# The seven 128x128 projections of a recurrent mixer as one fp32 product each, where three fp32r products of rounded parts stood

## The chip, the cores and the metric

One core of a Trainium2 chip runs the whole kernel. The metric is device time in microseconds of one execution; before the change the median of three runs is 784.83 us (784.66 to 788.44).

## The reference, cut to what matters

`xn` is the layer norm of an input of 16 sequences x 256 tokens x 128 channels. Two branches read it, and the output is `x + s * silu(cur)`.

```
# branch s, the mixer
xx  = prev_token(xn) - xn
lin = lambda mix, W: (xn + xx * mix) @ W.T          # six of these: r, w, k, v, a, g
r, alpha, g = sigmoid(lin(..)); decay = exp(-softplus(lin(..))); k = tanh(lin(..)); v = lin(..)
state = state * decay + alpha * k * v               # a scan over the tokens
mixed = r * state
s   = (group_norm(mixed) * gn_w + gn_b) * g @ W_out.T + b_out      # the seventh product
# branch cur, four rounds of four experts of width 512
for rnd in range(4):
    cw  = top-2 softmax weights of cur @ Wg[rnd] + bg[rnd]
    cur = cur + sum_e cw[e] * (gelu(cur @ W1[e] + b1[e]) @ W2[e] + b2[e])
```

All of it is fp32. The weights of the seven products are 128x128.

## The kernel before, in words

The 4096 tokens are cut into 8 blocks of 512 (two sequences each), with the channels on the partitions. The experts are run in 128 steps: step s is expert s % 4 of turn s // 4, and a turn is one block in one round. One step is `up` (four hidden tiles) and `down` (their sum into one bank). TensorE's program is one loop over the steps: `up(s + 1)`, `down(s)`, then what else belongs to step s (L1220 to L1236).

Each operand of `up` and `down` is an fp32r tensor, and each fp32 product is made of three fp32r products of 512 columns. For `v` and a weight `w`, `v_hi` is `v` rounded to fp32r and `v_lo = v - v_hi`; `mm_high` (L1079, L1080) multiplies `v_hi` by `w_hi` and by `w_lo`, and `mm_low` (L1083) multiplies `v_lo` by `w_hi`, all three into one PSUM bank. So one `up` is 12 matmuls and one `down` is 12. ScalarE takes each of the four hidden banks with a gelu (L465) and rounds pairs of them (L471), VectorE makes their low parts (L759) and weighs a finished `down` into `tmp` (L773), and GpSimd's queue adds `tmp` to `cur` by a DMA (L415).

The mixers lie between the steps. Mixer m (block m) begins at step 15 + 14 m, and `JOB_AT` gives the step within the mixer at which each of its seven products is made: 0 (w), 1 (a), 2 (k), 3 (v), 5 (r), 6 (g), 12 (the output product, J_S). That makes 8 x 7 = 56 products. For each of the first six, `mixer_input` on VectorE makes `xm` (L836, 128x512) and `parts` makes `part_hi` (L822) and `part_lo` (L824) from it; for the seventh, `mixer_gate` makes `gn` (L892), and `parts` splits that. `project` (L1193 to L1206) is TensorE's side and stands at the end of its step: three matmuls into `p_bank` (`pb`), of which the first waits for `part_ready` and `p_empty`, and the third for `part_ready` again. ScalarE takes `p_bank` (L477, L482) and VectorE takes it for v (L846). The parts have two buffers in turn; the weights' parts `pj_hi`, `pj_lo`, `wo_hi` and `wo_lo` are made once, at steps 13 and 14 (`high_mixw`, `low_mixw`), from copies that were loaded into a part of `xn_t` not yet in use. The SyncE queue therefore holds the copy of block 4 into `xn_t` back until `mixw_low`.

Two other uses of TensorE matter below. The router's logits (L1189) are plain fp32 products already: nine batches of two or four matmuls, each 512 columns against a weight of 32 columns, that go to different 32-partition parts of `r_bank`. And the normalised input is turned by fp32 transposes of 128 columns against the full 128-column identity (L1091, L1102).

Of the kernel before, what the change touches and what calls it, by code (L numbers as in the profile page):

```python
# [5 lines left out]
D = 128  # L6
SEQS, LEN = 16, 256
# [4 lines left out]
NB = TOK // BLK  # L12
# [79 lines left out]
def mixer_gated_experts(nc, x, proj_t, mixes, wout_t, chan_vecs, wg, bg, w1, b1, w2, b2, cw_scratch, out):  # L92
# [7 lines left out]
    with ExitStack() as ctx:  # L100
# [13 lines left out]

        w1_hi, w1_lo = sb("w1_hi", [128, E, F], f32r), sb("w1_lo", [128, E, F], f32r)
        w2_hi, w2_lo = sb("w2_hi", [128, E * FT, D], f32r), sb("w2_lo", [128, E * FT, D], f32r)
        pj_hi, pj_lo = sb("pj_hi", [128, 6, D], f32r), sb("pj_lo", [128, 6, D], f32r)
        wo_hi, wo_lo = sb("wo_hi", [128, D], f32r), sb("wo_lo", [128, D], f32r)
        wg_c = sb("wg_c", [128, R, E])

        wg_p = sb("wg_p", [128, R, RP])
# [26 lines left out]


        NG = 4 * GRP  # L150
        xx, xm = sb("xx", [128, 2, LEN]), sb("xm", [128, 2, LEN])
        part_hi, part_lo = sb("part_hi", [128, 2, 2, LEN], f32r), sb("part_lo", [128, 2, 2, LEN], f32r)
        dec, u, kt, rt, gt, st = (sb(n, [128, 2, LEN]) for n in ("dec", "u", "kt", "rt", "gt", "st"))

        st_blk, cen, sq, mn = dec, kt, u, rt
# [14 lines left out]

        w1_raw = cw_b[:, 1, :].rearrange("p (e f) -> p e f", e=E)
        w2_raw = [(th, xr)[e // 2][:, e % 2, :].rearrange("p (t h) -> p t h", h=D) for e in range(E)]
        proj_raw = xn_t[:, 8:11, 1:LEN + 1]
        wo_raw = xn_t[:, 11, 1:D + 1]

        hb = [bank(f"h_bank{i}") for i in range(FT)]
        yb = [bank(f"y_bank{i}") for i in range(2)]
# [11 lines left out]
        b1_loaded, first_turned, first_high = sem("b1_loaded"), sem("first_turned"), sem("first_high")  # L189
        dve_consts = sem("dve_consts")  # L190
        made, gates_padded, edge_zeroed = sem("made"), sem("gates_padded"), sem("edge_zeroed")
        w1_high, w2_high, mixw_high = sem("w1_high"), sem("w2_high"), sem("mixw_high")
        w1_low, w2_low, mixw_low = sem("w1_low"), sem("w2_low"), sem("mixw_low")
        rstd_ready = sem("rstd_ready")
        xn_first, xn_ready = sem("xn_first"), sem("xn_ready")
        xn_copied = sem("xn_copied")
# [60 lines left out]
        def _(sp):  # L257
# [27 lines left out]
                load_x(c)  # L285
            sp.dma_start(vec[:, :], chan_vecs).then_inc(small_loaded, DMA)
            sp.dma_start(mix[:, :], mixes).then_inc(small_loaded, DMA)
            sp.dma_start(proj_raw, proj_t.rearrange("d (k j) -> d k j", k=3)).then_inc(mixw_loaded, DMA)
            sp.dma_start(wo_raw, wout_t).then_inc(mixw_loaded, DMA)

            def copy_block(b):

                if b < BY_PE:
                    sp.wait_ge(p_empty, b + 1)
                else:
                    sp.wait_ge(cur_placed, b - BY_PE + 1)
                sp.wait_ge(edge_zeroed, 1)
                if b == NB // 2:
                    sp.wait_ge(mixw_low, 2)
                sp.dma_start(xn_t[:, 2 * b:2 * b + 2, 1:LEN + 1],  # L300
                             cur[:, block_of(b)].rearrange("p (b t) -> p b t", b=2)).then_inc(xn_copied, DMA)

# [115 lines left out]
        def _(act):  # L418
# [10 lines left out]
                act.wait_ge(w2_loaded[e], DMA)  # L429
                nc.scalar.activation(w2_hi[:, e * FT:(e + 1) * FT, :], w2_raw[e], ACT.Copy).then_inc(w2_high, 1)  # L430

            def high_mixw():
                act.wait_ge(mixw_loaded, DMA * MIXW)
                nc.scalar.activation(pj_hi[:, :, :].rearrange("p (a k) j -> p a (k j)", a=3), proj_raw,
                                     ACT.Copy).then_inc(mixw_high, 1)
                nc.scalar.activation(wo_hi[:, :], wo_raw, ACT.Copy).then_inc(mixw_high, 1)

            def scale_block(b):

                group = [b in blocks for blocks in NORM_GROUPS].index(True)  # L440
# [78 lines left out]
            for s in range(STEPS):  # L519
                if s == 1:  # L520
                    high_w1(3)
                elif s == 8:
                    router_tanh(1)
                elif s == 13:
                    act.wait_ge(small_loaded, DMA * SMALL)
                    high_mixw()
                elif s == 14:
                    router_tanh(2)
                for m, stage in mixers_at(s):
                    take(m, stage)  # L530
                for b, stage in end_stages_at(s):
                    if stage == "tanh" and b < NB - 2:
                        end_tanh(b)

                def between():
                    if s < E - 1:
                        high_w2(s + 1)
                    for b in at_step(NORM_SCALE, s):
                        scale_block(b)
                    for n in at_step(LOGITS_AT, s - 2):  # L540
                        if n >= 3:
                            router_tanh(n)
                    if (NB - 2, "tanh") in end_stages_at(s):
                        end_tanh(NB - 2)

                def late():
                    if s == 0:
                        router_tanh(0)

                if s + 1 < STEPS:  # L550
                    hidden(s + 1, between, late)
# [13 lines left out]
        def _(dve):  # L565
# [73 lines left out]
            def low_w2(e):  # L639
# [1 line left out]
                dve.wait_ge(w2_high, e + 1)  # L641
                nc.vector.tensor_tensor(w2_lo[:, h, :], w2_raw[e], as_f32(w2_hi[:, h, :]),
                                        ALU.subtract).then_inc(w2_low, 1)

            def low_mixw():
                dve.wait_ge(mixw_high, 2)
                nc.vector.tensor_tensor(pj_lo[:, :, :].rearrange("p (a k) j -> p a (k j)", a=3), proj_raw,
                                        as_f32(pj_hi[:, :, :]).rearrange("p (a k) j -> p a (k j)", a=3),
                                        ALU.subtract).then_inc(mixw_low, 1)
                nc.vector.tensor_tensor(wo_lo[:, :], wo_raw, as_f32(wo_hi[:, :]), ALU.subtract).then_inc(mixw_low, 1)  # L650

            def split_first():

# [160 lines left out]
                dve.wait_ge(half_combined, n + 1)  # L814
                nc.vector.tensor_tensor(last, last, part, ALU.add).then_inc(half_added, 1)

            def parts(m, job, src):

                turn = len(JOBS) * m + job
                if turn >= 2:  # L820
                    dve.wait_ge(p_full, BY_PE + turn - 1)
                nc.vector.tensor_scalar(part_hi[:, turn % 2, :, :], src, 1.0, None, ALU.mult).then_inc(part_ready, 1)  # L822
                dve.wait_ge(part_ready, 2 * turn + 1)
                nc.vector.tensor_tensor(part_lo[:, turn % 2, :, :], src, as_f32(part_hi[:, turn % 2, :, :]),  # L824
                                        ALU.subtract).then_inc(part_ready, 1)

            def mixer_input(m, job):

                xs = xn_t[:, 2 * m:2 * m + 2, :]
                if job == J_W:  # L830
                    dve.wait_ge(xn_copied, DMA * (m + 1))
                    link(nc.vector.tensor_tensor(xx[:, :, :], xs[:, :, 0:LEN], xs[:, :, 1:LEN + 1], ALU.subtract))
                k = KINDS[job]
                if len(JOBS) * m + job > 0:
                    dve.wait_ge(part_ready, 2 * (len(JOBS) * m + job))
                link(nc.vector.scalar_tensor_tensor(out=xm[:, :, :], in0=xx[:, :, :], scalar=mix[:, k:k + 1],  # L836
                                                    in1=xs[:, :, 1:LEN + 1], op0=ALU.mult, op1=ALU.add))
                parts(m, job, xm[:, :, :])

            def mixer_values(m):  # L840

# [47 lines left out]
            def mixer_gate(m):  # L889

                dve.wait_ge(p_empty, p_job(m, J_G) + 1)
                link(nc.vector.scalar_tensor_tensor(out=gn[:, :, :], in0=gt[:, :, :], scalar=1.0, in1=gn[:, :, :],  # L892
                                                    op0=ALU.add, op1=ALU.mult))
                parts(m, J_S, gn[:, :, :])

            def end_scaled(b):

# [61 lines left out]
            for s in range(STEPS):  # L959

                if s == 1:
                    split_cur(1)
                elif s == 2:
                    norm_root(NORM_GROUPS[1])
                elif s == 3:
                    norm_stats(NORM_GROUPS[2][0:2])
                elif s == 6:
                    norm_spread(NORM_GROUPS[2])
                    norm_root(NORM_GROUPS[2])
                elif s == 7:  # L970
                    router_scores(1)
                elif s == 8:
                    router_gates(1)
                elif s == 13:
                    router_scores(2)
                elif s == 14:
                    router_gates(2)
                    low_mixw()
                    nc.vector.tensor_scalar(gnw4[:, :], vec[:, 0:1], 0.25, None, ALU.mult)
                    nc.vector.tensor_scalar(gnb2[:, :], vec[:, 1:2], 0.5, None, ALU.mult).then_inc(dve_consts, 1)  # L980
                    dve.wait_ge(dve_consts, 1)
# [95 lines left out]
        def _(pe):  # L1077
# [115 lines left out]
            def project(m, job):  # L1193

                turn = len(JOBS) * m + job
                if turn == 0:
                    pe.wait_ge(mixw_low, 2)
                if job == J_S:
                    w_hi, w_lo = wo_hi[:, :], wo_lo[:, :]
                else:  # L1200
                    w_hi, w_lo = pj_hi[:, KINDS[job], :], pj_lo[:, KINDS[job], :]
                pe.wait_ge(part_ready, 2 * turn + 1)
                pe.wait_ge(p_empty, p_job(m, job))
                mm_high(pb[:, :], w_hi, w_lo, part_hi[:, turn % 2, :, :])
                pe.wait_ge(part_ready, 2 * turn + 2)
                mm_low(pb[:, :], w_hi, part_lo[:, turn % 2, :, :]).then_inc(p_full, 1)  # L1206

            pe.wait_ge(made, 3)
            for _ in range(WARM_UP):
# [71 lines left out]
```

## Time and profile before

| what | before |
|---|---|
| median of 3 runs | 784.83 us (784.66 to 788.44) |
| profiled execution, first to last instruction (span) | 782.9 us |
| granted TensorE clock, mean of the span | 1.000 |
| PE busy | 777.2 us, 99% |
| DVE busy | 689.3 us, 88% |
| ACT busy | 641.1 us, 82% |
| POOL busy | 115.2 us, 15% |

The profiled execution has no device time of its own in the records; beside its span stand the three times of the runs, whose median is 1.9 us above the span. PE is TensorE's matmul row, PEld its weight loads, DVE is VectorE, ACT ScalarE, POOL GpSimd, SP SyncE. The end of a matmul is modelled, and matmuls overlap: durations of 395 ns stand at starts 230 ns apart. What one costs TensorE is read from the starts. "TensorE clock 1.000" is the upper of its two levels, 2.4 GHz.

### The profile page before, as it was taken

Reading aid. Unit: us, or ns where it says so; the run is one execution under the profiler, and the core shown is the slowest. Engines: PE = TensorE matmul, PEld = TensorE weight load, DVE = VectorE, ACT = ScalarE, POOL = GpSimd, SP = SyncE. Lnnn points to the kernel's source line nnn. Section 1 sums busy time; section 2 is a strip of 40 time slices with the busy share of each in tenths; the row PEclk is TensorE's granted clock in tenths of the full one; section 3 lists DMA queues with packets and bytes.
Section 4 is the critical chain, followed back from the end, with each engine's and each line's share of the span. In section 5 each row is a group of like instructions: output and inputs, shape, how many; then the busy total and the mean of one; then the engine's idle time right before and its main releaser. Section 6 shows DMA issues by size and latency. Waiting matters only on the chain.

```text
span 782.9 us, 9951 instructions
## 1 busy us (share of the span) xinstructions
PE 777.2 (99%) x3392; PEld 619.2 (79%) x3392; DVE 689.3 (88%) x1096; ACT 641.1 (82%) x873; POOL 115.2 (15%) x141
## 2 busy tenths in 40 slices
PE   8999999999999999999999999999999999999998
PEld 6778788887888878888788887888877788888887
DVE  7999987899888889879899788987988989988998
ACT  7989888787888877888788877887877878888886
POOL 0122111111111111111111111111111111111110
PEclk9999999999999999999999999999999999999999
DMA  8467572332642416333154322643227434655453
GB/s 267 139 132 182 128 208 50 95 95 41 148 89 62 107 28 163 92 64 88 33 157 107 81 57 41 149 108 96 41 41 175 108 56 107 134 123 122 70 117 71
DMA packets 77010, 81.62 MB, mean 104 GB/s; under 512 B 48800, under 2 KB 54688, under 8 KB 72992
## 3 DMA queue, kind: packets, MB, share of 16 engines
q0 software_dynamic: 18624, 34.61, 25.8%
q1 hardware_dynamic: 57920, 46.11, 19.5%
q8 instruction: 27, 0.44, 0.2%
q10 hardware_dynamic: 416, 0.26, 0.1%
q14 instruction: 23, 0.19, 0.1%
HBM read 41.91 MB, written 3.93 MB: 59 GB/s over the span
## 4 chain that ended last, share of the span: by engine, by line
PE 95%; ACT 2%; DVE 2%; issue 0%; DMA 0%; DVEq 0%
PE h_bank L1079 15%; PE h_bank L1080 15%; PE h_bank L1083 15%; PE y_bank L1152 15%; PE y_bank L1142 15%; PE y_bank L1140 14%; PE p_bank L1079 2%; PE p_bank L1083 2%; PE p_bank L1080 2%; PE r_bank L1189 1%; ACT g L465 1%; ACT g_hi L471 1%; DVE g_lo L759 0%; DMA cur<-in_x 0%; DVE stats L600 0%
## 5 line engine op out<-in xcount | busy, mean ns | idle before, releaser
L465 ACT ACTIVATE g<-h_bank,b_c 128x512 f32<-128x512 f32 x512 | 329.3, 682 | 77.8 <-PE h_bank L1083 77.0
L759 DVE TENSOR_TENSOR g_lo<-g,g_hi 128x1024 fp32r<-128x1024 f32 x256 | 310.0, 1222 | 72.8 <-ACT g_hi L471 71.2
L471 ACT ACTIVATE g_hi<-g 128x1024 fp32r<-128x1024 f32 x256 | 271.8, 1062 | 8.1
L415 POOL DMA_DIRECT2D cur<-tmp x126 | 110.6, 878 | 642.4 <-DVE tmp L773 544.1
L1079 PE MATMUL h_bank<-cur_hi,w_hi 128*128 128x512 f32 x512 | 202.9, 396 | 0.2 <-ACT cur_hi L513 0.2
L1083 PE MATMUL h_bank<-cur_lo,w_hi 128*128 128x512 f32 x512 | 202.2, 395 | 0.0
L1080 PE MATMUL h_bank<-cur_hi,w_lo 128*128 128x512 f32 x512 | 202.1, 395 | 0.0
L1140 PE MATMUL y_bank<-g_hi,w_hi 128*128 128x512 f32 x504 | 196.2, 393 | 0.0
L1142 PE MATMUL y_bank<-g_hi,w_lo 128*128 128x512 f32 x488 | 193.6, 397 | 0.0
L1152 PE MATMUL y_bank<-g_lo,w_hi 128*128 128x512 f32 x504 | 137.9, 395 | 0.1
L1079 PEld LDWEIGHTS h_bank<-cur_hi,w_hi 128*128 128x128 f32 x512 | 96.2, 188 | 26.6 <-issue 3.8
L1083 PEld LDWEIGHTS h_bank<-cur_lo,w_hi 128*128 128x128 f32 x512 | 96.2, 188 | 23.3 <-DVE cur_lo L663 0.2
L1080 PEld LDWEIGHTS h_bank<-cur_hi,w_lo 128*128 128x128 f32 x512 | 96.3, 188 | 22.6
L1152 PEld LDWEIGHTS y_bank<-g_lo,w_hi 128*128 128x128 f32 x504 | 94.6, 188 | 23.1 <-DVE g_lo L759 0.5
L1140 PEld LDWEIGHTS y_bank<-g_hi,w_hi 128*128 128x128 f32 x504 | 94.7, 188 | 22.4 <-issue 0.8
L1142 PEld LDWEIGHTS y_bank<-g_hi,w_lo 128*128 128x128 f32 x488 | 91.7, 188 | 23.0
L773 DVE SCALAR_TENSOR_TENSOR tmp<-y_bank,b_c,cw_b 128x512 f32<-128x512 f32 x126 | 93.6, 743 | 0.0
L836 DVE SCALAR_TENSOR_TENSOR xm<-xx,mix,xn_t 128x512 f32<-128x512 f32 x48 | 35.7, 744 | 0.3
L824 DVE TENSOR_TENSOR part_lo<-xm,part_hi 128x512 fp32r<-128x512 f32 x48 | 33.2, 692 | 1.7
L708 DVE TENSOR_TENSOR cur_lo<-cur,cur_hi 128x512 fp32r<-128x512 f32 x31 | 21.5, 692 | 1.1
L822 DVE TENSOR_SCALAR part_hi<-xm 128x512 fp32r<-128x512 f32 x48 | 20.8, 434 | 1.6
L1079 PE MATMUL p_bank<-part_hi,pj_hi 128*128 128x512 f32 x48 | 19.3, 401 | 0.0
(153 smaller groups left out, 410.5 us busy)
## 6 DMA issues: line engine op xcount, KB each, us to landing
cur<-tmp POOLq DMA_DIRECT2D x126, 256.0 KB, 3.3
cw_b<-cw_scratch SPq DMA_DIRECT2D x31, 1024.0 KB, 5.2
xn_t<-cur SPq DMA_DIRECT2D x8, 256.0 KB, 3.1
cur<-in_x SPq DMA_DIRECT2D x7, 256.0 KB, 5.0
xr<-in_x SPq DMA_DIRECT2D x28, 64.0 KB, 3.4
out<-o SPq DMA_DIRECT2D x28, 64.0 KB, 2.1
xn_scratch<-o POOLq DMA_DIRECT2D x6, 256.0 KB, 3.0
xr<-xn_scratch SPq DMA_DIRECT2D x24, 64.0 KB, 2.5
```

The source lines that it names most:

```text
L415: pool.dma_start(cur[:, block_of(s // E)], tmp[:, s % SUMS, :], accum_op=ALU.add).then_inc(summed, DMA)
L465: nc.scalar.activation(g[:, gb, ft * BLK:(ft + 1) * BLK], hb[ft][:, :], ACT.Gelu_apprx_tanh, bias=b1_c[:, e * FT + ft:e * FT + ft + 1]).th ...
L471: nc.scalar.activation(g_hi[:, gb, h], g[:, gb, h], ACT.Copy).then_inc(g_hi_done, 1)
L759: nc.vector.tensor_tensor(g_lo[:, gb, h], g[:, gb, h], as_f32(g_hi[:, gb, h]), ALU.subtract).then_inc(g_lo_done, 1)
L773: nc.vector.scalar_tensor_tensor(out=tmp[:, s % SUMS, :], in0=yb[s % 2][:, :], scalar=b2_c[:, e:e + 1], in1=cw_b[:, q, e * BLK:(e + 1) * BLK],
L836: link(nc.vector.scalar_tensor_tensor(out=xm[:, :, :], in0=xx[:, :, :], scalar=mix[:, k:k + 1], in1=xs[:, :, 1:LEN + 1], op0=ALU.mult, op1 ...
L1079: nc.tensor.matmul(out_ap, w_hi, v_hi, start=True, stop=False)
L1080: nc.tensor.matmul(out_ap, w_lo, v_hi, start=False, stop=False)
L1083: return nc.tensor.matmul(out_ap, w_hi, v_lo, start=False, stop=True)
L1140: nc.tensor.matmul(yb[b][:, :], w2_hi[:, e * FT + ft, :], hi, start=(ft == 0), stop=False)
L1142: nc.tensor.matmul(yb[b][:, :], w2_lo[:, e * FT + ft, :], hi, start=False, stop=False)
L1152: last = nc.tensor.matmul(yb[b][:, :], w2_hi[:, e * FT + ft, :], g_lo[:, b, ft * BLK:(ft + 1) * BLK], start=False, stop=(ft == FT - 1))
```

## The change

The mixers' weights and inputs stay fp32, and each of the 56 products becomes one matmul instruction on plain fp32 operands. The rounding and subtracting go, on ScalarE and VectorE, with their buffers and two semaphores. `xm` has two buffers in their place, and `mixer_input` waits, before it writes one, for the product that read it last. The weights are loaded straight to `pj` and `wo`, and the copy of block 4 no longer waits for anything of the weights. The seventh product reads `gn` itself.

```
-        xx, xm = sb("xx", [128, 2, LEN]), sb("xm", [128, 2, LEN])
-        part_hi, part_lo = sb("part_hi", [128, 2, 2, LEN], f32r), sb("part_lo", [128, 2, 2, LEN], f32r)
+        xx, xm = sb("xx", [128, 2, LEN]), sb("xm", [128, 2, 2, LEN])
...
-            sp.dma_start(proj_raw, proj_t.rearrange("d (k j) -> d k j", k=3)).then_inc(mixw_loaded, DMA)
-            sp.dma_start(wo_raw, wout_t).then_inc(mixw_loaded, DMA)
+            sp.dma_start(pj[:, :, :].rearrange("p k j -> p (k j)"), proj_t).then_inc(mixw_loaded, DMA)
+            sp.dma_start(wo[:, :], wout_t).then_inc(mixw_loaded, DMA)
...
-                if b == NB // 2:
-                    sp.wait_ge(mixw_low, 2)
...
-            def high_mixw():
...
-            def low_mixw():
...
-            def parts(m, job, src):
-
-                turn = len(JOBS) * m + job
-                if turn >= 2:
-                    dve.wait_ge(p_full, BY_PE + turn - 1)
-                nc.vector.tensor_scalar(part_hi[:, turn % 2, :, :], src, 1.0, None, ALU.mult).then_inc(part_ready, 1)
-                dve.wait_ge(part_ready, 2 * turn + 1)
-                nc.vector.tensor_tensor(part_lo[:, turn % 2, :, :], src, as_f32(part_hi[:, turn % 2, :, :]),
-                                        ALU.subtract).then_inc(part_ready, 1)
...
-                if len(JOBS) * m + job > 0:
-                    dve.wait_ge(part_ready, 2 * (len(JOBS) * m + job))
-                link(nc.vector.scalar_tensor_tensor(out=xm[:, :, :], in0=xx[:, :, :], scalar=mix[:, k:k + 1],
-                                                    in1=xs[:, :, 1:LEN + 1], op0=ALU.mult, op1=ALU.add))
-                parts(m, job, xm[:, :, :])
+                turn = len(JOBS) * m + job
+                if turn >= 2:
+                    dve.wait_ge(p_full, BY_PE + turn - 1)
+                nc.vector.scalar_tensor_tensor(out=xm[:, turn % 2], in0=xx[:, :, :], scalar=mix[:, k:k + 1],
+                                               in1=xs[:, :, 1:LEN + 1], op0=ALU.mult, op1=ALU.add).then_inc(part_ready, 1)
...
-                parts(m, J_S, gn[:, :, :])
...
-                pe.wait_ge(part_ready, 2 * turn + 1)
-                pe.wait_ge(p_empty, p_job(m, job))
-                mm_high(pb[:, :], w_hi, w_lo, part_hi[:, turn % 2, :, :])
-                pe.wait_ge(part_ready, 2 * turn + 2)
-                mm_low(pb[:, :], w_hi, part_lo[:, turn % 2, :, :]).then_inc(p_full, 1)
+                pe.wait_ge(part_ready, turn + 1)
+                pe.wait_ge(p_empty, p_job(m, job))
+                if job == J_S:
+                    nc.tensor.matmul(pb[:, :], wo[:, :], gn[:, :, :], start=True, stop=True).then_inc(p_full, 1)
+                else:
+                    nc.tensor.matmul(pb[:, :], pj[:, KINDS[job], :], xm[:, turn % 2], start=True, stop=True).then_inc(p_full, 1)
```

TensorE's program around the first product (end of step 15, mixer 0, job w), before and then with the change. `y_bank` is the sum of `down(15)`, `h_bank` the first hidden tile of the next `up`.

```order
403 L1152 MATMUL y_bank<-g_lo,w_hi 128x512 [waits g_lo_done]
404 L1152 MATMUL y_bank<-g_lo,w_hi 128x512
405 L1079 MATMUL p_bank<-part_hi,pj_hi 128x512 [waits p_empty,part_ready,mixw_low]
406 L1080 MATMUL p_bank<-part_hi,pj_lo 128x512
407 L1083 MATMUL p_bank<-part_lo,pj_hi 128x512 [waits part_ready]
408 L1079 MATMUL h_bank<-cur_hi,w_hi 128x512 [waits gelu_done]
```

```order
402 L1120 MATMUL y_bank<-g_lo,w_hi 128x512
403 L1120 MATMUL y_bank<-g_lo,w_hi 128x512 [waits g_lo_done]
404 L1120 MATMUL y_bank<-g_lo,w_hi 128x512
405 L1171 MATMUL p_bank<-xm,pj 128x512 [waits p_empty,part_ready,mixw_loaded]
406 L1047 MATMUL h_bank<-cur_hi,w_hi 128x512 [waits gelu_done]
```

The product keeps its place between `down` and the next `up`; three instructions have become one, and one of their waits is gone. Nothing else in TensorE's program moves.

## Rows read from the trace of the kernel before

**Rows 1.** The page: span, busy time by engine, granted TensorE clock in 40 slices.
```profile
span 782.9 us, 9951 instructions
PE 777.2 (99%) x3392; PEld 619.2 (79%) x3392; DVE 689.3 (88%) x1096; ACT 641.1 (82%) x873; POOL 115.2 (15%) x141
...
PEclk9999999999999999999999999999999999999999
```
**Rows 2.** The waits: engine line, waited for: us in total, times, longest us.
```profile
ACT g L465 <- PE h_bank L1083: 77.0, 106, 2.8
DVE g_lo L759 <- ACT g_hi L471: 71.2, 97, 2.9
...
PEld p_bank L1083 <- DVE part_lo L824: 0.7, 2, 0.4
...
PE y_bank L1102 <- DVE o L940: 0.5, 1, 0.5
```
**Rows 3.** The chain in order of time (start us, us, engine, tile, line), plain steps.
```profile
672.75 0.93 PE y_bank L1152 x4
678.35 0.93 PE y_bank L1152 x4
```
**Rows 4.** The timeline, TensorE, a step with a product: start us, us, engine, operation.
```profile
353.17 0.39 PE L1079 MATMUL h_bank<-cur_hi,w_hi 128*128 128x512 f32 x1
...
358.77 0.39 PE L1079 MATMUL p_bank<-part_hi,pj_hi 128*128 128x512 f32 x1
...
359.23 0.40 PE L1083 MATMUL p_bank<-part_lo,pj_hi 128*128 128x512 f32 x1
359.46 0.39 PE L1079 MATMUL h_bank<-cur_hi,w_hi 128*128 128x512 f32 x1
```
**Rows 5.** The logits' line L1189: durations in ns (min/median/max), first and last start.
```profile
L1189 PE MATMUL r_bank<-cur,wg_p x64: 592/605/617, 16.5 to 600.4; 128*32 128x512 f32 x64
```
**Rows 6.** The timeline around the last batch of logits, TensorE.
```profile
598.88 1.10 PE L1152 MATMUL y_bank<-g_lo,w_hi 128*128 128x512 f32 x4
599.92 1.06 PE L1189 MATMUL r_bank<-cur,wg_p 128*32 128x512 f32 x8
600.91 0.50 PE L1079 MATMUL p_bank<-part_hi,wo_hi 128*128 128x512 f32 x1
601.25 0.40 PE L1080 MATMUL p_bank<-part_hi,wo_lo 128*128 128x512 f32 x1
```
**Rows 7.** The same place, the window cut at 600.2 us, with the weight loads.
```profile
599.92 0.16 PEld L1189 LDWEIGHTS r_bank<-cur,wg_p 128*32 128x32 f32 x8 [0.37 <-issue]
599.92 0.64 PE L1189 MATMUL r_bank<-cur,wg_p 128*32 128x512 f32 x4
```
**Rows 8.** The timeline around four fp32 transposes: matmuls, then weight loads.
```profile
12.97 0.39 PE L1083 MATMUL h_bank<-cur_lo,w_hi 128*128 128x512 f32 x1
13.21 0.60 PE L1091 MATMUL p_bank<-ident,o 128*128 128x128 f32 x4
13.56 0.48 PE L1079 MATMUL h_bank<-cur_hi,w_hi 128*128 128x512 f32 x1
13.88 0.39 PE L1080 MATMUL h_bank<-cur_hi,w_lo 128*128 128x512 f32 x1
...
12.97 0.59 PEld L1091 LDWEIGHTS p_bank<-ident,o 128*128 128x128 f32 x4
```
**Rows 9.** The groups by line and form: xcount, busy us, mean ns.
```profile
L824 DVE TENSOR_TENSOR part_lo<-xm,part_hi 128x512 fp32r<-128x512 f32 x48 | 33.2, 692 | 1.7
...
L822 DVE TENSOR_SCALAR part_hi<-xm 128x512 fp32r<-128x512 f32 x48 | 20.8, 434 | 1.6
```
**Rows 10.** The timeline, ACT, around one product of mixer 5.
```profile
456.66 0.60 ACT L477 ACTIVATE kt<-p_bank 128x512 f32<-128x512 f32 x1 [0.86 <-PE p_bank L1083]
```
**Rows 11.** The timeline, where TensorE waits for a part (mixer 6, job w).
```profile
611.74 0.75 DVE L836 SCALAR_TENSOR_TENSOR xm<-xx,mix,xn_t 128x512 f32<-128x512 f32 x1
...
613.01 0.19 PEld L1079 LDWEIGHTS p_bank<-part_hi,pj_hi 128*128 128x128 f32 x1 [0.42 <-DVE part_hi L822]
```

More of the change, by code:

```diff
@@ L116, in mixer_gated_experts @@
         w2_hi, w2_lo = sb("w2_hi", [128, E * FT, D], f32r), sb("w2_lo", [128, E * FT, D], f32r)
-        pj_hi, pj_lo = sb("pj_hi", [128, 6, D], f32r), sb("pj_lo", [128, 6, D], f32r)
-        wo_hi, wo_lo = sb("wo_hi", [128, D], f32r), sb("wo_lo", [128, D], f32r)
+        pj, wo = sb("pj", [128, 6, D]), sb("wo", [128, D])
         wg_c = sb("wg_c", [128, R, E])
@@ L172, in mixer_gated_experts @@
         w2_raw = [(th, xr)[e // 2][:, e % 2, :].rearrange("p (t h) -> p t h", h=D) for e in range(E)]
-        proj_raw = xn_t[:, 8:11, 1:LEN + 1]
-        wo_raw = xn_t[:, 11, 1:D + 1]
         hb = [bank(f"h_bank{i}") for i in range(FT)]
@@ L191, in mixer_gated_experts @@
         made, gates_padded, edge_zeroed = sem("made"), sem("gates_padded"), sem("edge_zeroed")
-        w1_high, w2_high, mixw_high = sem("w1_high"), sem("w2_high"), sem("mixw_high")
-        w1_low, w2_low, mixw_low = sem("w1_low"), sem("w2_low"), sem("mixw_low")
+        w1_high, w2_high = sem("w1_high"), sem("w2_high")
+        w1_low, w2_low = sem("w1_low"), sem("w2_low")
         rstd_ready = sem("rstd_ready")
@@ L430, in high_w2 @@
                 nc.scalar.activation(w2_hi[:, e * FT:(e + 1) * FT, :], w2_raw[e], ACT.Copy).then_inc(w2_high, 1)
-            def high_mixw():
[L433 to L436, printed above, removed]
             def scale_block(b):
@@ L525, in _ @@
                     act.wait_ge(small_loaded, DMA * SMALL)
-                    high_mixw()
                 elif s == 14:
@@ L643, in low_w2 @@
                                         ALU.subtract).then_inc(w2_low, 1)
-            def low_mixw():
[L646 to L650, printed above, removed]
             def split_first():
@@ L891, in mixer_gate @@
                 dve.wait_ge(p_empty, p_job(m, J_G) + 1)
-                link(nc.vector.scalar_tensor_tensor(out=gn[:, :, :], in0=gt[:, :, :], scalar=1.0, in1=gn[:, :, :],
-                                                    op0=ALU.add, op1=ALU.mult))
-                parts(m, J_S, gn[:, :, :])
+                nc.vector.scalar_tensor_tensor(out=gn[:, :, :], in0=gt[:, :, :], scalar=1.0, in1=gn[:, :, :],
+                                               op0=ALU.add, op1=ALU.mult).then_inc(part_ready, 1)
             def end_scaled(b):
@@ L977, in _ @@
                     router_gates(2)
-                    low_mixw()
                     nc.vector.tensor_scalar(gnw4[:, :], vec[:, 0:1], 0.25, None, ALU.mult)
@@ L1196, in project @@
                 if turn == 0:
-                    pe.wait_ge(mixw_low, 2)
+                    pe.wait_ge(mixw_loaded, DMA * MIXW)
+                pe.wait_ge(part_ready, turn + 1)
+                pe.wait_ge(p_empty, p_job(m, job))
                 if job == J_S:
-                    w_hi, w_lo = wo_hi[:, :], wo_lo[:, :]
+                    nc.tensor.matmul(pb[:, :], wo[:, :], gn[:, :, :], start=True, stop=True).then_inc(p_full, 1)
                 else:
-                    w_hi, w_lo = pj_hi[:, KINDS[job], :], pj_lo[:, KINDS[job], :]
-                pe.wait_ge(part_ready, 2 * turn + 1)
-                pe.wait_ge(p_empty, p_job(m, job))
-                mm_high(pb[:, :], w_hi, w_lo, part_hi[:, turn % 2, :, :])
-                pe.wait_ge(part_ready, 2 * turn + 2)
-                mm_low(pb[:, :], w_hi, part_lo[:, turn % 2, :, :]).then_inc(p_full, 1)
+                    nc.tensor.matmul(pb[:, :], pj[:, KINDS[job], :], xm[:, turn % 2], start=True, stop=True).then_inc(p_full, 1)
             pe.wait_ge(made, 3)
```

## The prediction

> **What bounds the kernel now.** I read the page first, then the waits, the chain, and the timeline at four places. The page [rows 1] has TensorE busy for 777.2 of 782.9 us and its granted clock full in every slice, so it runs at its upper level of 2.4 GHz throughout. Busy time alone proves little, since matmuls overlap in the trace. The waits [rows 2] settle it: the largest wait of ScalarE's gelu is 77.0 us on `up`'s last product, and the largest of VectorE's is 71.2 us on ScalarE, which itself waited for TensorE. TensorE's own waits are the other way round: outside the warm-up at the start the largest is 0.5 us, and its weight loads waited 0.7 us for `part_lo` in the whole run. Everything waits for TensorE, and TensorE for almost nothing.
>
> What it does in that time is regular. A plain step is 5.60 us (672.75 to 678.35, [rows 3]), which is 24 matmuls 0.233 us apart. A step with a product is 6.29 us (353.17 to 359.46, [rows 4]), and the product takes the 0.69 of difference, 358.77 to 359.46: three fp32r matmuls 0.23 us apart, with no gap on either side. So the kernel's time is a sum of TensorE's start-to-start distances. 128 steps at 5.60 are 716.8 us, and 56 products at 0.69 are 38.6 us; the rest of the 782.9 us is nine batches of logits, the start and the end. Whatever lengthens a product lengthens the kernel by 56 times that.
>
> **The change, part by part.**
>
> *The products on TensorE.* 56 x 3 fp32r matmuls go, 56 x 0.69 = 38.6 us. 56 plain fp32 ones of 512 columns against a full 128x128 weight come. The trace has no such product. Its nearest relation is the logits' matmul: plain fp32 and 512 columns too, but against 32 columns of weight. It tells two things. First, one instruction of the program leaves two records: 32 logits matmuls are x64 [rows 5], and a batch of four is x8 [rows 6]. Second, how far apart the two passes start. The last of the eight ends at 599.92 + 1.06 = 600.98 and took 0.59, so it started at 600.39. The last of the first four ends at 599.92 + 0.64 = 600.56 [rows 7] and took 0.617 [rows 5], so it started at 599.94. The distance is 0.45 us, against 0.23 for an fp32r matmul of as many columns: two passes, each at about half the rate. I take 2 x 0.45 = 0.90 us a product, 0.21 more than now, or 56 x 0.21 = **+11.8 us**.
>
> The bounds of a pass: a pass's record is 0.592 long without a load ahead of it [rows 5] and an fp32r matmul's is 0.39 [rows 4], so 0.23 + 0.20 = 0.43 from below; twice the fp32r distance, 0.46, from above. That is 0.86 to 0.92 a product and +9.5 to +12.9 us.
>
> The Trainium skill ("FP8 and Floating Point Precision", section on TensorE precision notes) says that true fp32 takes four passes through the array. The trace shows two records, not four; with four passes at the fp32r distance of 0.23 the sum would be 4 x 0.23 - 0.69 = 0.23 more a product, 12.9 us, which is the upper bound above, so rule and rows speak alike against this change, which leaves three.
>
> *The edges of a product.* Here the shapes part company. Around a batch of logits TensorE loses more than the two passes. The last matmul ahead of it starts at 598.88 + 1.10 - 0.39 = 599.59, so the next was due at 599.82; the logits start at 599.92. After them the first fp32r matmul starts at 600.91 and the second at 601.25, 0.34 later instead of 0.23 [rows 6]: its weight load was not drawn ahead of the running matmul, and 0.11 of it lies open. The loads of the logits were not drawn ahead either: they begin with the matmul, after 0.37 us in which the load row was idle "for nothing" [rows 7]. All in all the batch takes 601.02 - 599.82 = 1.20 us. The fp32 transposes, with a full 128-column weight, lose nothing of this kind [rows 8]: the load starts with the last fp32r matmul at 12.97, the first transpose follows at 13.21, and after four of them the stream is back in step (13.88 - 0.23 = 13.65, so 0.44 us for four). The open edges thus belong either to the 32-column weight or to the fp32 passes. The shape is that of the transposes, so I take none.
>
> The Trainium skill ("TensorEngine Tiling (Array Packing)", section on key properties) states that changing the tiling mode drains the array. By that rule the logits' edges come from their 32-column tiles, and a 128x128 product has none; without it the price would be that of the second rival below.
>
> *VectorE.* For each of 48 products 0.434 + 0.692 us go [rows 9], 54 us in all, and as much each for the 8 output products, 9 us; also one subtraction of the weights. VectorE is ahead of TensorE and only waits longer for ScalarE [rows 2]: nothing. The exception is a place where TensorE waits for a part: at 613.01 its load waited 0.42 us for `part_hi` though `xm` was ready at 611.74 + 0.75 = 612.49 [rows 11]; with the 0.7 us for `part_lo` [rows 2] that is 1.1 us in three waits. A load can be drawn 0.23 us ahead, so about 1.1 - 3 x 0.23 = 0.4 us of it cost time. These go, since `xm` alone is ready earlier: **-0.4 us**, between 0 and -1.1.
>
> *The new wait of VectorE.* It now waits for product n-2 before it writes `xm`, as it did before it wrote `part_hi`. That product ended at least a step, 5.60 us, earlier. The `g_lo` behind it in the queue sees nothing. Nothing.
>
> *ScalarE and SyncE.* Two roundings of weights go. ScalarE takes `p_bank` after 0.86 us of waiting for TensorE [rows 10]; the product ends 0.21 us later, so the wait is 1.07, and the next gelu's bank, which TensorE fills only after the product, moves by as much. Nothing. The copy of block 4 and the gate transfers queued behind it on SP are freed from a wait; none of them is what TensorE waits for. Nothing. If the cover were gone, the 0.6 us of taking `p_bank` would be what came late.
>
> *The sum.* 11.8 - 0.4 = +11.4 us on the profiled span, 794.3 us; on the median of 784.83 (1.9 us above the span, which stays), **796.2 us**. The bounds together are +9.5 - 1.1 = 8.4 to +12.9, or 793.2 to 797.7 us.
>
> **The rivals.**
>
> *The edges come with fp32* (no full-tile rule, as at the logits). Then a product costs 1.20 - 0.02 (the four of a batch start 0.02 apart in all) = 1.18 us, or 0.08 more where the open load ahead of it is of 128 columns (0.11) and not of 32 (0.617 - 0.592 = 0.03): 0.49 to 0.57 more than now, 27 to 32 us, 812 to 816 us. For it: mode and length are those of the logits. Against it: the transposes.
>
> *Only one load lies open.* Each product pays 0.11 us for a load that cannot be drawn ahead on one side: 6.2 us on top, 802.4 us. Nothing shows it but the logits' far edge.
>
> *Full-rate passes, the other side.* Half rate may belong to the 32-column weight, and a full 128x128 fp32 pass may start 0.23 us after another as the fp32r ones do. Then a product is 0.46, which is 0.23 less than now, at each of the 56 places at the end of a step: -12.9 - 0.4, 771.5 us. It decides from 0.345 us a pass (0.69 / 2) downwards. For it: no row shows half rate in an fp32 instruction with a full-width weight. Against it: the transposes, 0.11 us apart for 128 columns [rows 8], are as slow as half rate would make them (0.45 / 4), though their loads could be the cause of that; and the width of a weight gives no reason for the rate of the moving columns.
>
> *Nearly nothing.* Passes of 0.31 to 0.38 us would give a time within 0.5% of now, which is about what a measurement of this kernel can tell from no change. No row has such a distance. That the change does not do what it says is excluded by the program's order: one matmul stands where three stood.
>
> **How the numbers follow.** Forecast 0.74; edges with fp32 0.11; one open load 0.07; full-rate passes 0.05; nearly nothing 0.03. The range takes the forecast's bounds and the open load (0.81 together), with a little for the medians: 792.5 to 803.0 us. Slower by over 0.5% (above 788.8) are the first three, 0.92; within it 0.03; faster (below 780.9) 0.05.
>
> **What would show it.** Right: two records of `p_bank<-xm,pj` for each product, x96 and x16 with the output products, their starts about 0.45 us apart; a step with a product 6.5 us long and a plain one still 5.60; the weight load of the first pass starting with the matmul before it; DVE busy near 625 us and PE still 99%. Wrong: first `up` matmul after a product more than 0.95 us after the product's first record (edges), the second `up` matmul 0.34 after the first (an open load), or passes 0.23 apart (faster). Plain steps of another length would make the whole sum wrong.

## The result, and the profile after

| | before | after |
|---|---|---|
| median of four runs each | 784.79 us (784.66 to 788.44) | 791.87 us (791.85 to 793.41) |
| ratio, 95% interval | | 1.0089 [1.0067, 1.0111] |
| span of the profiled execution | 782.9 us | 790.0 us |

The change costs 7.1 us. Its sign was forecast, its size was not: 11.4 us had been predicted, and 791.87 lies just under the range of 792.5 to 803.0. TensorE's granted clock stayed at its upper level, 0.999 to 1.000 in every run of this document.

The page of the changed kernel, answering to [rows 1]:

```profile
span 790.0 us, 9668 instructions
PE 784.8 (99%) x3336; PEld 610.7 (77%) x3336; DVE 629.2 (80%) x982; ACT 639.9 (81%) x871; POOL 113.4 (14%) x141
...
PEclk9999999999999999999999999999999999999999
```

VectorE lost 60.1 us of work and the kernel is slower. Its waits (engine line, waited for: total us, times, longest) show where the 60 us went, against [rows 2]:

```profile
DVE g_lo L739 <- ACT g_hi L459: 138.8, 139, 3.5
...
ACT g L453 <- PE h_bank L1051: 78.0, 106, 3.0
PEld h_bank L1047 <- issue: 17.3, 61, 0.8
...
PEld h_bank L1048 <- issue: 13.4, 56, 0.2
```

VectorE now waits 138.8 us for ScalarE instead of 71.2. The wait for `part_lo` is gone, and no wait for `xm` has come in its place. New are 56 idle stretches "for nothing" in the row of weight loads ahead of each of the first two matmuls of `up` (the kernel before had 5, 3.8 us in all): a pass of an fp32 product takes 0.43 us, longer than the 0.23 from one load to the next elsewhere, and the load row stands idle meanwhile.

One product, TensorE's timeline (start us, us, engine, operation), answering to [rows 4]:

```profile
366.96 1.09 PE L1120 MATMUL y_bank<-g_lo,w_hi 128*128 128x512 f32 x4
367.89 1.02 PE L1171 MATMUL p_bank<-xm,pj 128*128 128x512 f32 x2
368.35 0.80 PE L1047 MATMUL h_bank<-cur_hi,w_hi 128*128 128x512 f32 x1
368.98 0.39 PE L1048 MATMUL h_bank<-cur_hi,w_lo 128*128 128x512 f32 x1
```

and its loads:

```profile
367.66 0.42 PEld L1171 LDWEIGHTS p_bank<-xm,pj 128*128 128x128 f32 x2
368.32 0.19 PEld L1047 LDWEIGHTS h_bank<-cur_hi,w_hi 128*128 128x128 f32 x1 [0.24 <-issue]
```

The first pass's load begins at 367.66, 0.23 ahead of the product, and the second's at 367.66 + 0.42 - 0.19 = 367.89, ahead of its own pass at 368.32, so no load lies open on the near side. On the far side the row of the first `up` matmul misleads: it is put at 368.35 with 0.80 us, twice its usual length. I read it as queueing behind the second pass: the matmul behind it starts at 368.98, one distance of 0.23 after a start of the first at 368.75, and e2 bears the reading out. So the product took 368.75 - 367.89 = 0.86 us in the stream. In 52 of the 56 products the second pass starts 0.428 to 0.434 us after the first; in the four that follow a batch of logits it is 0.533, the 0.11 of open load that the first fp32r matmul behind the logits pays in the kernel before too [rows 6].

### The profile page after: what moved, and what is told of

It is laid out like the page before. It is cut to its first block, busy times and chain, and to the rows that moved or that the text cites. A ratio compares the mean times of both kernels' runs of the same rounds, so it can differ in the third digit from the quotient of the medians.

```text
span 790.0 us, 9668 instructions
## 1 busy us (share of the span) xinstructions
PE 784.8 (99%) x3336; PEld 610.7 (77%) x3336; DVE 629.2 (80%) x982; ACT 639.9 (81%) x871; POOL 113.4 (14%) x141
## 4 chain that ended last, share of the span: by engine, by line
PE 95%; ACT 2%; DVE 2%; issue 0%; DMA 0%; DVEq 0%
PE h_bank L1047 15%; PE h_bank L1051 14%; PE h_bank L1048 14%; PE y_bank L1120 14%; PE y_bank L1108 14%; PE y_bank L1110 14%; PE p_bank L1171 5%; PE r_bank L1157 1%; PE p_bank L1169 1%; ACT g L453 1%; ACT g_hi L459 1%; DVE g_lo L739 0%; DMA cur<-in_x 0%; DVE stats L587 0%; ACT o L436 0%
## 5 line engine op out<-in xcount | busy, mean ns | idle before, releaser
L739 DVE TENSOR_TENSOR g_lo<-g,g_hi 128x1024 fp32r<-128x1024 f32 x256 | 311.0, 1223 | 141.1 <-ACT g_hi L459 138.8
L1047 PE MATMUL h_bank<-cur_hi,w_hi 128*128 128x512 f32 x512 | 225.1, 440 | 0.2 <-ACT cur_hi L501 0.2
L409 POOL DMA_DIRECT2D cur<-tmp x126 | 108.7, 863 | 651.6 <-DVE tmp L753 499.8
L1171 PE MATMUL p_bank<-xm,pj 128*128 128x512 f32 x96 | 49.3, 595 | 0.0
L1171 PEld LDWEIGHTS p_bank<-xm,pj 128*128 128x128 f32 x96 | 17.9, 189 | 6.5 <-issue 2.5
L686 DVE TENSOR_SCALAR cur_hi<-cur 128x512 fp32r<-128x512 f32 x31 | 13.5, 434 | 0.5
```

What stands on the lines that cost most here:

```text
L409: pool.dma_start(cur[:, block_of(s // E)], tmp[:, s % SUMS, :], accum_op=ALU.add).then_inc(summed, DMA)
L739: nc.vector.tensor_tensor(g_lo[:, gb, h], g[:, gb, h], as_f32(g_hi[:, gb, h]), ALU.subtract).then_inc(g_lo_done, 1)
L1047: nc.tensor.matmul(out_ap, w_hi, v_hi, start=True, stop=False)
L1171: nc.tensor.matmul(pb[:, :], pj[:, KINDS[job], :], xm[:, turn % 2], start=True, stop=True).then_inc(p_full, 1)
```

## The experiments

Each batch ran beside the kernel before, whose median was 784.88 us for e1 to e4, 784.65 for e5 to e11 and 784.75 for e12 to e15.

### e1: VectorE's work put back

```
+                dve.wait_ge(part_ready, turn + 1)
+                link(nc.vector.tensor_scalar(spare_hi[:, :, :], src, 1.0, None, ALU.mult))
+                Own.n += 1
+                nc.vector.tensor_tensor(spare_lo[:, :, :], src, as_f32(spare_hi[:, :, :]), ALU.subtract).then_inc(dve_step, 1)
...
+                spare_parts(turn, xm[:, turn % 2])
...
+                spare_parts(len(JOBS) * m + J_S, gn[:, :, :])
```

> The changed kernel with VectorE's old work put back beside it: it still rounds each product's input and subtracts (128x512, 56 times each) into two spare buffers that nobody reads. TensorE still makes one fp32 product. Theory A (only TensorE's own sum counts; VectorE's relief was worth at most the waits for parts, 0.4 to 0.6 us): 791.9 to 792.5 us, plain steps inside the mixers 5.58 us as in the changed kernel. Rival B (the lighter VectorE is why plain steps inside the mixers fell from 5.60 to 5.58 us and the product's steps cost 0.02 less than two passes): those steps go back to 5.60 and the time rises by 1.5 to 2.5 us, to 793.5 us or more.

Measured: 792.17 us, ratio to before 1.0097 [1.0082, 1.0112], against 1.0089 without that work. VectorE is as full as it was:

```profile
span 790.5 us, 9780 instructions
...
PE 784.7 (99%) x3336; PEld 610.0 (77%) x3336; DVE 688.1 (87%) x1094; ACT 639.7 (81%) x871; POOL 115.3 (15%) x141
```

Theory A held. 59 us of VectorE's work bring 0.3 us here, which these runs can't tell from nothing, and the traces put none of it into TensorE's stream: from step 10 on, well ahead of the first product, 116 of 117 step lengths are those of the changed kernel within 2 ns and one within 4. The two executions differ in the steps before. In mixer 6's first product, where TensorE had waited for `part_hi` [rows 11], no wait returned either: the last four `down` matmuls begin at 618.15, and the product follows in step, four distances of 0.23 later.

```profile
618.15 1.09 PE L1130 MATMUL y_bank<-g_lo,w_hi 128*128 128x512 f32 x4
619.09 1.02 PE L1181 MATMUL p_bank<-xm,pj 128*128 128x512 f32 x2
```

So what the change gave back there came from TensorE no longer needing the parts, not from an emptier VectorE. The plain steps that the change brought to 5.57 to 5.59 us stayed there and did not go back to 5.60, which excludes rival B.

### e2: every product twice

```
+                    nc.tensor.matmul(pb[:, :], pj[:, KINDS[job], :], xm[:, turn % 2], start=True, stop=True)
                     nc.tensor.matmul(pb[:, :], pj[:, KINDS[job], :], xm[:, turn % 2], start=True, stop=True).then_inc(p_full, 1)
... (the output product likewise, here and in e3 and e4)
```

> The changed kernel with each of the 56 fp32 products issued twice into the same bank (the second overwrites the first; the result is the same). Theory A (a product is two passes of 0.4275 us and has no edges): the second copy costs 0.855 each, 47.9 us, 839.8 us in all. Rival B (part of what a product costs lies at its edges, against the fp32r stream, and the passes are cheaper): less, 45 us or under, with passes of the second copy closer than 0.42 us.

Measured: 839.94 us, 48.07 more than the changed kernel, or 0.858 us a product. The timeline has the two copies 107.70 - 106.84 = 0.86 apart:

```profile
106.84 1.02 PE L1172 MATMUL p_bank<-xm,pj 128*128 128x512 f32 x2
107.70 1.02 PE L1173 MATMUL p_bank<-xm,pj 128*128 128x512 f32 x2
```

A second copy costs as much as the first one takes in the stream. A full-width fp32 product among fp32r matmuls has no edges that one could see, and its price is two passes of 0.428.

### e3: the product in four tiles of 32 weight columns

```
-                    nc.tensor.matmul(pb[:, :], pj[:, KINDS[job], :], xm[:, turn % 2], start=True, stop=True).then_inc(p_full, 1)
+                    for c in range(0, D, 32):
+                        last = nc.tensor.matmul(pb[c:c + 32, :], pj[:, KINDS[job], c:c + 32], xm[:, turn % 2], start=True, stop=True)
+                    last.then_inc(p_full, 1)
```

> The changed kernel with each product cut into four matmuls of 32 weight columns that go to the four 32-partition parts of the bank, as the logits do. Same data, same fp32 passes. Theory A (the open edges of the logits come from their 32-column tiles): 1.18 to 1.20 us a product as at the logits against 0.855, +18 to +19 us, 810 to 811 us, and the first weight load no longer starts with the matmul before it. Rival B (the logits' edges have another cause, their waits or their place in the step): four tiles run side by side and only their 0.02 us of stagger is added, 793 us.

Measured: 809.24 us, 17.4 more than the changed kernel, 0.31 a product. The same operands and the same fp32 passes now show the logits' picture [rows 6]:

```profile
105.97 1.10 PE L1120 MATMUL y_bank<-g_lo,w_hi 128*128 128x512 f32 x4
107.00 1.07 PE L1174 MATMUL p_bank<-xm,pj 128*32 128x512 f32 x8
108.00 0.51 PE L1047 MATMUL h_bank<-cur_hi,w_hi 128*128 128x512 f32 x1
108.34 0.39 PE L1048 MATMUL h_bank<-cur_hi,w_lo 128*128 128x512 f32 x1
```

Theory A held in kind; the time is 0.8 us under its 810. The 0.31 is a mean over unequal places: the four products behind a batch of logits cost nothing more than in the changed kernel, since they share the edges of the logits, and the others cost 0.34 each, or 0.855 + 0.34 = 1.20 us, as at the logits. Of the difference, 0.6 us came back in other distances of the stream (below). It is the tiles that open the edges of an fp32 product.

### e4: the product in two halves of 256 columns

```
+                    for a in range(2):
+                        last = nc.tensor.matmul(pb[:, a * LEN:(a + 1) * LEN], pj[:, KINDS[job], :], xm[:, turn % 2, a, :], start=True, stop=True)
+                    last.then_inc(p_full, 1)
```

> The changed kernel with each product cut into two matmuls of 256 columns (one per sequence). Theory A (an fp32 pass costs its columns at half rate and nothing else, 512 / 1.2 GHz = 0.427): four passes of 0.2135, the time stays at 791.9 within 0.5. Rival B (each pass pays something fixed, like the 0.01 to 0.02 us that fp32r matmuls stand above their columns at full rate): two more passes a product, 0.02 to 0.04 us each product, +1 to +2 us.

Measured: 792.21 us, 0.34 more than the changed kernel. The four passes start 0.215 us apart, half of 0.428 and not more:

```profile
106.75 1.02 PE L1174 MATMUL p_bank<-xm,pj 128*128 128x256 f32 x4
```

By these two lengths a pass costs 0.83 ns a column, two ticks of the 2.4 GHz that the clock was granted (512 / 1.2 = 427 ns), and 1 to 2 ns of its own. The fp32r matmuls around it do not run so close to their columns: 0.233 for 512, where one tick a column would be 0.213.

### e5, e12, e13, e14: to whom the open edges belong

Four kernels put one narrow matmul of 32 weight columns and 512 moving columns ahead of each product. The product overwrites its result.

```
# e5, kernel before:    fp32r, columns 0 to 31
+                nc.tensor.matmul(pb[0:32, :], w_hi[:, 0:32], part_hi[:, turn % 2, :, :], start=True, stop=True)
# e12 and e13, changed kernel: fp32, columns 0 to 31 and 32 to 63 (here e13)
+                stored_w = wo[:, 32:64] if job == J_S else pj[:, KINDS[job], 32:64]
+                nc.tensor.matmul(pb[32:64, :], stored_w, gn[:, :, :] if job == J_S else xm[:, turn % 2], start=True, stop=True)
# e14, changed kernel: bf16 constants
+                nc.tensor.matmul(pb[32:64, :], small_w[:, :], small_v[:, :], start=True, stop=True)
```

> The kernel before with one fp32r matmul of 32 weight columns (512 columns, into 32 partitions of the bank, overwritten afterwards) put ahead of each product's three. Theory A (the open edges belong to the change between 32 and 128 weight columns, whatever the type): 0.23 us of matmul and about 0.32 us of edges, 56 x 0.55 = 31 us, 816 us. Rival B (edges need fp32 passes as well as narrow tiles): 56 x 0.2325 = 13.0 us, 797.9 us.

> The changed kernel with one fp32 matmul of 32 weight columns into partitions 0 to 31 of the bank ahead of each product (overwritten by it). Theory A (open edges need fp32 passes and a narrow weight together): two passes, 0.855, and about 0.30 of open edges around the narrow one, 56 x 1.16 = 65 us, 857 us. Rival B (a narrow weight at column 0 is no change of mode, as the fp32r one of e5 was none): 56 x 0.855 = 47.9 us, 839.8 us.

> The same with the narrow fp32 matmul going to partitions 32 to 63 of the bank. If e12 has no edges and this one has, the edges come from a tile that does not begin at column 0 (857 us). If both have or both lack them, the place makes no difference.

> The changed kernel with a bf16 matmul of 32 weight columns and 512 columns of constants into partitions 32 to 63 ahead of each product (overwritten by it). Theory A (the edges come with the column tile, whatever the type): 0.2135 + 0.30, 56 x 0.51 = 29 us, 821 us. Rival B (they need fp32 passes): 56 x 0.2135 = 12 us, 804 us.

| | time, us | above its base, each of 56 | at the product alone | passes themselves | edges |
|---|---|---|---|---|---|
| e5 fp32r | 795.43 | 10.8 / 56 = 0.19 | 0.23 | 0.23 | none |
| e12 fp32 at column 0 | 857.30 | 65.4 / 56 = 1.17 | 1.18 | 0.855 | 0.32 |
| e13 fp32 at column 32 | 857.28 | 65.4 / 56 = 1.17 | 1.18 | 0.855 | 0.32 |
| e14 bf16 at column 32 | 822.25 | 30.4 / 56 = 0.54 | 0.52 | 0.21 | 0.31 |

The base is the kernel before for e5 and the changed kernel for the others. "At the product alone" is by how much the stretch from the last matmul of `down` to the second of `up` grew in the trace, in the 50 places with neither logits nor a wait for parts beside them. The two columns differ because every such insertion also moves the distances of the matmuls around it: in e5 these fell from 232.9 to 232.3 ns, in e14 they rose from 232.5 in the changed kernel to 233.2, 2.3 us in all. The 0.21 of e14 is what its bf16 matmul adds behind the logits, where the edges are open already.

For e5 theory A failed: a narrow fp32r matmul is just another one in the stream, its starts 0.24 and 0.23 from its neighbours. The time of rival B was 2.5 us too high as well, mostly because the stream around it grew quicker.

```profile
106.98 0.39 PE L1204 MATMUL p_bank<-part_hi,pj_hi 128*32 128x512 f32 x1
107.22 0.39 PE L1079 MATMUL p_bank<-part_hi,pj_hi 128*128 128x512 f32 x1
```

For fp32 and bf16 the edges came, wherever the tile lay. e14's matmul is due 0.23 after the last of four that began at 105.92, at about 106.85, but starts at 106.94, and the two fp32 passes behind it are 1.13 long together where they are 1.02 in the changed kernel, since the first carries its own open load:

```profile
105.92 1.09 PE L1124 MATMUL y_bank<-g_lo,w_hi 128*128 128x512 f32 x4
106.94 0.39 PE L1174 MATMUL p_bank<-small_v,small_w 128*32 128x512 bf16 x1
107.26 1.13 PE L1178 MATMUL p_bank<-xm,pj 128*128 128x512 f32 x2
```

So neither fp32 passes alone nor a narrow weight alone open the edges. A matmul of 32 weight columns does in fp32 and in bf16. The narrow fp32r matmul behaves as if it were no column tile, though the trace has it as 128*32 too; why is not shown by any run. The Trainium skill ("TensorEngine Tiling (Array Packing)", section on key properties) says that changing the tiling mode drains the array. By that rule a pair of changes costs something: the fp32 and bf16 runs agree and give 0.31 to 0.34 us for it, e5 does not show it.

### e8 and e10: one and four fp32r matmuls a product

```
# e8
-                mm_high(pb[:, :], w_hi, w_lo, part_hi[:, turn % 2, :, :])
-                pe.wait_ge(part_ready, 2 * turn + 2)
-                mm_low(pb[:, :], w_hi, part_lo[:, turn % 2, :, :]).then_inc(p_full, 1)
+                nc.tensor.matmul(pb[:, :], w_hi, part_hi[:, turn % 2, :, :], start=True, stop=True).then_inc(p_full, 1)
# e10
+                nc.tensor.matmul(pb[:, :], w_hi, part_hi[:, turn % 2, :, :], start=True, stop=True)
                 mm_high(pb[:, :], w_hi, w_lo, part_hi[:, turn % 2, :, :])
```

> The kernel before with only the first of each product's three fp32r matmuls (the rounded input by the rounded weight; the two products with the low parts are left out, VectorE still makes the low part). Theory A (TensorE alone sets the time down here too): 112 matmuls of 0.2325 us less, -26.0 us, 758.8 us. Rival B (VectorE, busy for up to 6.15 of the 6.29 us of a step with a product, becomes the bound in those steps, now 5.83 us long for TensorE): 765 to 775 us, with waits of TensorE's loads for the input's part or g_lo.

> The kernel before with the first fp32r matmul of each product issued twice (four instead of three; the result is the same). It prices one fp32r matmul inside the stream and asks for the rhythm of the starts, which is 229 and 238 ns in turn in the mixers of the kernel before (mean 233.3) and a longer cycle of mean 232.3 in the changed kernel. Theory A (the slow rhythm comes from the odd number of fp32r matmuls in a step with a product): it goes, 784.9 + 13.0 - 2.3 = 795.6 us. Rival B (it does not depend on the count): it stays, 797.9 us.

e8: 757.86 us, 26.8 less than before (expected 26.0). TensorE is still the bound when a product is a third of its size, VectorE still waits for ScalarE:

```profile
DVE g_lo L759 <- ACT g_hi L471: 45.2, 55, 2.4
```

e10: 795.56 us, 10.9 more than before, where 13.0 is the price of the matmuls themselves (0.234 each at the product). With the fourth matmul some 2 us came back elsewhere. The chain shows it in plain steps of the mixers (start us, us), 5.57 to 5.58 apart in e10 and 5.60 in the kernel before [rows 3]:

```profile
247.62 0.92 PE y_bank L1152 x4
253.19 0.94 PE y_bank L1152 x4
258.77 0.93 PE y_bank L1152 x4
```

The starts have two rhythms. In the kernel before they are mostly 229 and 238 ns in turn, mean 233.3; in e10 and in the changed kernel mostly a longer cycle with values of 228 to 241, mean 232.3. All of these kernels have steps of both kinds: of 65 plain steps, 40 are 5.60 us long in the kernel before and 10 in the changed one. Over all fp32r distances of 512 columns (those under 245 ns) the mean is 232.9 ns before (3185 of them), 232.6 after (2970), 232.4 in e10 (3241).

### e11: only the output products whole

```
+                if job == J_S:
+                    nc.tensor.matmul(pb[:, :], wo[:, :], gn[:, :, :], start=True, stop=True).then_inc(p_full, 1)
+                    return
                 mm_high(pb[:, :], w_hi, w_lo, part_hi[:, turn % 2, :, :])
... (wo is loaded plain, and VectorE leaves out the parts of gn)
```

> The kernel before with only the 8 output products as one fp32 product each, the 48 others as three fp32r matmuls. Theory A (each product costs 0.16 us more on its own account, plus what its step's other matmuls give back by a quicker rhythm): 8 x 0.16 = 1.3 us at most, 785.9 to 786.2 us. Rival B (the first product that is changed brings a cost of its own, such as a changed mode that is paid once per change): more than 787 us.

Measured: 785.89 us, ratio 1.0015 [1.0006, 1.0024], 1.24 us for 8 products, 0.155 each. The price is paid per product, and nothing that one could see is paid once.

### e15: the slow rhythm, by the number of matmuls

```
-                mm_low(pb[:, :], w_hi, part_lo[:, turn % 2, :, :]).then_inc(p_full, 1)
+                for a in range(2):
+                    last = nc.tensor.matmul(pb[:, a * LEN:(a + 1) * LEN], w_hi, part_lo[:, turn % 2, a, :], start=False, stop=(a == 1))
+                last.then_inc(p_full, 1)
```

> The kernel before with the third fp32r matmul of each product cut into two of 256 columns, so that a step with a product has 28 matmuls and not 27, for the same columns (256 columns take 0.116 to 0.118 each). Theory A (the slow rhythm of 233.3 ns comes from the count of matmuls in these steps, as e10 and e5 point): steps fall to a mean of 232.3 to 232.5 a matmul, 1 to 2 us less, 782.8 to 783.8 us, quicker than the kernel before. Rival B (an extra instruction only costs): 784.7 to 785.5 us.

Measured: 785.36 us, ratio 1.001 [1.0001, 1.0019]. Theory A failed: there are 28 matmuls in a step with a product, as in e10, and the plain steps stay 5.60 apart (49 of 64).

```profile
246.03 0.93 PE y_bank L1152 x4
251.63 0.93 PE y_bank L1152 x4
257.23 0.93 PE y_bank L1152 x4
```

The hope of a version that beats the kernel before rested on this run, and it fell with it. What chooses the rhythm stays open: VectorE's load (e1) and the mere count of matmuls (e15) are excluded, and what stands at the product does change it. In e3, with fp32 tiles, hardly a plain step is 5.60 us long; in e14, with one bf16 matmul, all 65 are.

## Why the prediction missed

**What bounds the kernel** was right. TensorE's starts add up to the time in every run: twice the product costs twice (e2), a third of it gives two thirds back (e8), 59 us of VectorE's work are worth nothing that one can tell (e1).

**The size of a pass** was the step that failed first: "The distance is 0.45 us ... I take 2 x 0.45 = 0.90 us a product". A pass takes 0.428, a product 0.855. The 0.45 was read at the logits, from the first pass to the second, and the first pass there carries the open load of its own 32 weight columns. The rows had the size of it: 0.617 against 0.592 [rows 5], 0.025 us; the two passes of one logits matmul start 0.453 apart in the trace, and that less 0.025 is the 0.428 of the changed kernel. The text used these 0.03 us for a rival and not for its own term. That is 2 x (0.45 - 0.4275) x 56 = 2.5 us too many. The lower bound, "0.43 from below", was the value. Four passes at the fp32r distance would have been 0.92 us a product; the trace has two records and 0.855.

**The size of what goes** was right, 0.69: in nanoseconds a step with a product is 6293 and a plain one 5600, so 0.693. The product therefore costs 0.855 - 0.693 = 0.162 us more, and 56 of them 9.1 us, not 11.8.

**A term was missing**: that other matmuls keep their price ("a plain one still 5.60") was put at nothing without a reason. This step took the time out of the range. The 3224 matmuls that are not products stand in both traces in the same order, so they can be held against each other one by one. Away from the products, 2937 distances of fp32r matmuls fell from a mean of 232.85 ns to 232.45, 1.2 us in all. "Plain steps of another length would make the whole sum wrong" named the sign to look for. The chain has them 5.60 apart before and 5.58 after, at the same place:

```profile
239.31 0.93 PE y_bank L1152 x4
244.91 0.93 PE y_bank L1152 x4
250.51 0.93 PE y_bank L1152 x4
```

```profile
241.01 0.93 PE y_bank L1120 x4
246.59 0.93 PE y_bank L1120 x4
252.17 0.92 PE y_bank L1120 x4
```

**The waits for parts**, 0.4 us, were a little larger, 0.6, and inside their bounds. The place at mixer 6 in the kernel before:

```profile
612.63 0.39 PE L1152 MATMUL y_bank<-g_lo,w_hi 128*128 128x512 f32 x1
613.01 0.50 PE L1079 MATMUL p_bank<-part_hi,pj_hi 128*128 128x512 f32 x1
613.35 0.39 PE L1080 MATMUL p_bank<-part_hi,pj_lo 128*128 128x512 f32 x1
613.74 0.50 PE L1083 MATMUL p_bank<-part_lo,pj_hi 128*128 128x512 f32 x1
614.07 0.39 PE L1079 MATMUL h_bank<-cur_hi,w_hi 128*128 128x512 f32 x1
```

The four starts are 0.38, 0.34, 0.39 and 0.33 us apart where 0.23 is the rule, 0.51 us in all, and the third wait, in the next step, cost 0.10. Each wait also left 0.10 to 0.11 of the load behind it open, which "A load can be drawn 0.23 us ahead" did not count. After, both products are in step.

The sum by what was measured is 9.1 - 0.6 - 1.2 = 7.3 us, and the start, the logits and the end gave 0.2 us back: 7.1. The first two terms alone, 8.5 us, would give 793.3, inside the range; what took the time out of it is the change of rhythm, and its cause stays open.

**The edges** were costed at nothing, by the shape of the transposes, and that was right (e2). (The price without that rule is the first rival's; the text points to the second by mistake.) The rival "the edges come with fp32" is refuted by e2 and e3 together; "only one load lies open" by the load at 367.66. The one trace of it is where a product follows the logits directly: there its load is open by 0.11 us, as that of an fp32r matmul is in the kernel before, so it costs nothing in the comparison. "Full-rate passes" is refuted by 0.428.

**The range** was too narrow at the bottom because its bounds held the price of a pass and the waits, and nothing for the rest of the stream. That rest is 691 us of fp32r distances after the change, where a part in a thousand is 0.7 us, and this one moved by 1.7 in a thousand.

## What to carry to other kernels

One plain fp32 product of full width costs 0.855 us for 512 columns and three fp32r products cost 0.69, so the split product is 0.16 us cheaper on TensorE, and a kernel like this one, with VectorE time to spare, should keep it. When the price of an operation is borrowed from a smaller relative in the trace, take the relative's own extras off first: here the record lengths of its first and second pass differ by what must not be carried over. In this kernel, which one engine fills to 99%, work removed from the others was worth nothing that could be told, and a change of a thousandth in that engine's usual distance is worth as much as the waits that one can see. To price a change, match the two traces operation by operation: a mean over all places hides shared edges and what the rest of the stream gives back.

## What the runs showed of the hardware that was not expected

- A matmul of 32 weight columns among full-width ones opens edges in fp32 (0.32 us for one, 0.34 for four tiles) and in bf16 (0.31); in fp32r it does not.
- The start of an fp32r matmul behind an fp32 pass is recorded at the pass's side, 0.46 us after the first pass, with a length of 0.80; only the record after it tells when it ran.
- The distance of fp32r matmuls of 512 columns has two rhythms, mean 233.3 and 232.3 ns, and a few other matmuls can change which of them holds for hundreds of others: 40 of 65 plain steps were slow before, 10 with fp32 products, all 65 with one bf16 matmul ahead of each.
